# Ahead of each gather GpSimd waits for the memset two back instead of for the newest one

## What is computed

```python
sparse_embed = emb_tables[field_idx[None, :], x_sparse]          # 512 x 26 x 64
z = sparse_embed.reshape(B, N_FIELDS * K)
gram = jnp.einsum('bik,bjk->bij', sparse_embed, sparse_embed)
inner = gram[:, iu, ju]                                          # 325 pairs
dnn_in = jnp.concatenate([x_dense, z, inner], axis=-1)           # 512 x 2002
h = jax.nn.relu(dnn_in @ w1 + b1)
out = jax.nn.sigmoid(h @ w2 + b2)
```

## Time and profile before

| | us |
|---|---|
| median of 3 runs | 212.64 (212.23 to 212.67) |
| span of the profiled execution, first to last instruction | 209.4 |
| what lies around the span (median less span) | 3.2 |
| TensorE busy in the span | 200.7 |
| GpSimd busy in the span | 128.2 |
| time GpSimd's gathers sat idle behind the memset | 26.3 |

### The profile page before, as it was taken

How to read it: one execution, slowest core, us unless ns; L and a number is a source line. 1 busy time by engine, 2 the same in 40 slices (tenths; PEclk the granted TensorE clock), 3 DMA queues, 4 the chain that set the end, 5 groups by cost and what they waited for, 6 DMA issues and landing times.

```text
span 209.4 us, 3900 instructions
## 1 busy us (share of the span) xinstructions
PE 200.7 (96%) x1340; PEld 162.1 (77%) x1340; DVE 148.3 (71%) x346; ACT 129.7 (62%) x257; POOL 128.2 (61%) x210
## 2 busy tenths in 40 slices
PE   8999989699999999999999899999999999999993
PEld 8966867578777788876888688888888888788882
DVE  3666675498936779869668899574976897673473
ACT  2765464397937848977387736685999947542201
POOL 5887888888787887858878788878785000000000
PEclk9999999999999999999999999999999999999999
DMA  5388999977493831336786566978897178023100
GB/s 155 91 269 257 322 297 349 363 223 256 127 299 92 278 107 29 116 79 161 253 312 215 141 202 180 338 222 226 270 300 219 67 202 292 9 46 56 30 0 0
DMA packets 15388, 39.00 MB, mean 186 GB/s; under 512 B 3881, under 2 KB 5281, under 8 KB 15369
## 3 DMA queue, kind: packets, MB, share of 16 engines
q1 hardware_dynamic: 11688, 35.27, 52.0%
q0 software_dynamic: 3328, 3.41, 7.7%
q10 hardware_dynamic: 353, 0.08, 0.2%
HBM read 37.71 MB, written 0.69 MB: 183 GB/s over the span
## 4 chain that ended last, share of the span: by engine, by line
PE 65%; POOL 16%; DMA 6%; DVE 5%; issue 5%; ACT 2%; DVEq 0%; POOLq 0%; ACTq 0%
PE slot L1080 19%; PE slot L1083 18%; PE slot L1086 18%; POOL E L824 14%; DMA E<-emb,row_idx 5%; PE slot L1040 4%; PE slot L1070 2%; PE slot L1071 2%; PE slot L1072 2%; DVE G L978 2%; POOL pace L832 2%; DVE w_lo L930 1%; ACT w_hi L848 1%; DMA x_idx<-idx 1%; DVE slot L1004 1%
## 5 line engine op out<-in xcount | busy, mean ns | idle before, releaser
L824 POOL DMA_INDIRECT E<-emb,row_idx x104 | 110.5, 1063 | 31.7 <-POOL pace L832 26.3
L930 DVE TENSOR_TENSOR w_lo<-w_raw,w_hi 128x500 fp32r<-128x500 f32 (+6 forms) x128 | 80.2, 671 | 10.4 <-ACT w_hi L848 9.6
L848 ACT CAST w_hi<-w_raw 128x1000 fp32r<-128x1000 f32 (+6 forms) x64 | 65.5, 1029 | 27.3 <-DMA w_raw<-w 18.8
L1080 PE MATMUL slot<-w_hi,x_hi 128*128 128x500 f32 (+5 forms) x236 | 75.1, 399 | 3.6 <-ACT x_hi L874 2.6
L1083 PE MATMUL slot<-w_lo,x_hi 128*128 128x500 f32 (+5 forms) x236 | 72.8, 389 | 0.0
L1086 PE MATMUL slot<-w_hi,x_lo 128*128 128x500 f32 (+5 forms) x236 | 72.6, 389 | 0.0
L1080 PEld LDWEIGHTS slot<-w_hi,x_hi 128*128 128x128 f32 (+2 forms) x236 | 43.0, 189 | 15.9 <-ACT x_hi L874 6.1
L1086 PEld LDWEIGHTS slot<-w_hi,x_lo 128*128 128x128 f32 (+2 forms) x236 | 44.5, 189 | 9.2
L1083 PEld LDWEIGHTS slot<-w_lo,x_hi 128*128 128x128 f32 (+2 forms) x236 | 44.5, 189 | 9.2
L879 ACT COPY ET<-T 32x128 f32<-32x128 f32 (+4 forms) x89 | 32.5, 366 | 2.0
L947 DVE STREAM_TRANSPOSE T<-E 128x256 f32<-128x256 f32 x24 | 10.6, 443 | 21.1 <-DMA E<-emb,row_idx 21.0
(11 more groups left out here) (39 smaller groups left out, 80.4 us busy)
## 6 DMA issues: line engine op xcount, KB each, us to landing
w_raw<-w SPq DMA_DIRECT2D x32, 501.0 KB, 5.2
w_raw<-w SPq DMA_DIRECT2D x32, 500.0 KB, 4.6
E<-emb,row_idx POOLq DMA_INDIRECT x104, 4.0
w_all<-w SPq DMA_DIRECT2D x1, 1001.0 KB, 7.3
gram_dram<-G SPq DMA_DIRECT2D x8, 84.5 KB
x_in<-gram_dram SPq DMA_DIRECT2D x8, 42.0 KB
x_in<-G SPq DMA_DIRECT2D x4, 58.5 KB
x_in<-G SPq DMA_DIRECT2D x4, 19.5 KB
```

The lines of the kernel that those rows point to most:

```text
L824: nc.gpsimd.indirect_dma_start(out=E[:, k % ER, j, :], out_offset=None, in_=emb_rows, in_offset=bass.IndirectOffsetOnAxis(ap=row_idx[:, at ...
L848: nc.scalar.copy(w_parts(m)[0], w_source(m)).then_inc(w_hi_ready, 1)
L930: nc.vector.tensor_tensor(lo[:, cols], w_source(m)[:, cols], hi[:, cols].bitcast(F32), ALU.subtract)\
L1080: nc.tensor.matmul(acc[q], xh, hi[:, cols[q]], start=first, stop=False)
```

## The change

Three edits. The tile `pace` gets two halves, used in turn. The wait on `paced` moves from behind the memset to ahead of it, and asks for the memset before the last one; so between a memset and the gather behind it there is no wait. And the planner's assumed time from gather to gather goes from 1.50 to 1.40 us.

```diff
             for _ in range(GROUP_GATHERS[ARRIVALS[k][1]]):
-                pool_at += 1.25 if k < 2 else 1.50
+                pool_at += 1.25 if k < 2 else 1.40
                 g_issued.append(pool_at)
...
-        pace = sb("pace", [P, PACE], F32)
+        pace = sb("pace", [P, 2, PACE], F32)
...
                     if at > SOON:
-                        nc.gpsimd.memset(pace[:], 0.0).then_inc(paced, 1)
-                        pool.wait_ge(paced, at - SOON)
+                        if at > SOON + 2:
+                            pool.wait_ge(paced, at - SOON - 2)
+                        nc.gpsimd.memset(pace[:, at % 2], 0.0).then_inc(paced, 1)
```

## The result

The changed kernel takes 210.41 us (median of 18 runs) against 212.41 of the kernel before in the same comparison; the ratio is 0.9909, with a 95% interval of 0.9886 to 0.9933. So it is faster by about 1.9 us, where 2.7 were forecast. The profiled execution has a span of 207.4 us, before 209.4. The ratios leave out executions that are over 1.5% above the fastest of their kernel, here mostly ones whose mean TensorE clock is 0.982 to 0.992, so for a kernel that often loses clock the ratio looks better than its median.

What follows compares the result with a forecast made beforehand. TensorE, busy 200.7 of 209.4 us, was taken as the bound, idling for late gather arrivals up to k11. Gains 1.5 (k4, k5) + 1.5 (later boundaries) - 0.3 (piece 34) = 2.7 us: 212.64 to 209.9, range 208.7 to 212.9, chance 0.53.

Steps and rivals of the forecast that it cites:

- The interval: GpSimd's quiet gather-to-gather time: from 1.39 to 1.285 us, a gain of 0.10 a gather, bounds 1.25 and 1.42.
- interval stays: Rival at GpSimd: the memset's 0.17 replaces the wait's cost, interval within 0.02 of 1.39; 212.6 us, chance 0.13.
- interval grows: Rival at GpSimd: the gather's 0.30 starts at the memset's end, each interval 0.03 longer; 213.8 us, chance 0.11.
- all of 0.27 goes: Last rival, at GpSimd: gathers follow memsets at once, 1.12 us apart; 208.5 us, chance 0.05.
- What it brings at k4 and k5: TensorE's waits for gather arrivals k4 (0.8 lost) and k5 (2.1 lost): earlier gathers win 1.5 us by k5.
- the landing doesn't move: Rival: the DMA queue, not GpSimd, sets when k4 and k5 land; first 1.5 us lost, 211.4 us, chance 0.18.
- k9 and k11: TensorE's waits at arrivals k9 and k11, bound by gathers: losses of 0.3 and 0.25 us go.
- k6 and k10: x_hi casts for arrivals k6 and k10 move ahead of a weight cast: losses of 0.36 and 0.4 us go.
- k8: Arrival k8, three weight casts staying ahead: about 0.35 of 0.5 us stays, 0.15 goes.
- the boundaries: TensorE's idle time where arrivals k6, k8, k9, k10 and k11 begin: 1.5 us won in sum.
- The new lists: Reordered operations from the planner's 1.40: k6 0.36, k10 0.4 and k8 0.15 us go, against 0.3 lost at piece 34.
- The loss: Two copies into X24 ahead of weight pieces 32 to 34 delay piece 34's w_lo: 0.3 us, bounds 0 and 0.5.

Runs made afterwards that it cites:

- e3: The changed kernel with memsets only behind the first eight paced gathers; ratio to the kernel before 0.9886 (0.9833 to 0.9939), quiet interval 1.25 us.
- e1: The changed kernel with the planner's old 1.50, so the new wait and halved tile with the old lists; ratio to the kernel before 0.9906 (0.9867 to 0.9945).
- e2: The kernel before with only the planner's number set to 1.40, so new lists with the old wait; ratio 1.0229 (1.0183 to 1.0275), 4.9 us slower.
- second trace: The changed kernel run again, unedited, on one chip with three other kernels; 210.54 us, ratio to the kernel before 0.994 (0.9904 to 0.9976).
- e7: The changed kernel with x_hi of (3,6) ahead of weight cast hi 38 in ScalarE's list; ratio to the kernel before 0.9891 (0.9854 to 0.9928).
- e4: The changed kernel with the 1 MB load of w2_all issued behind load 20 instead of load 12; ratio to the kernel before 0.9962 (0.9925 to 0.9998).
- e6: The kernel before with the 1 MB load of w2_all moved behind load 29; ratio to the unedited kernel before 1.0131 (1.0093 to 1.0169).
- e10: The changed kernel with x_hi of (3,6) ahead of hi 38, hi 54 moved earlier, few memsets, w2_all in its old place; 208.25 us, ratio to before 0.9831.

## Why the prediction was right, and where its sizes were off

*The interval* came out at 1.28 against 1.285 taken; both bounds (1.25 and 1.42) are excluded for the kernel as it is, and e3 shows the 0.30 as a start of the gather's own. The rivals "interval stays", "interval grows" and "all of 0.27 goes" fall by this one number. By the Trainium skill, "GPSIMD Engine Reference", section Instruction dispatch, completion of a Pool instruction does not hold back the next one. The trace agrees so far: at 1.28, and not 1.42, the gather's start of 0.30 is not held back until the memset has ended. The 1.12 that the last rival made of this rule left that start out. The advice of "Perfetto Trace Analysis" in the Trainium skill, section GPSIMD Engine Instruction, to go by start-to-start spacing, held: the spacing gave 1.285, the lengths 1.12.

*What it brings at k4 and k5* is the term that was mis-sized: 1.5 forecast, 0.9 in the trace (k5 from 38.45 to 37.57). The cause is that I used the quiet gain of 0.10 for every interval. From the 5th to the 20th gather the mean is (30.57 - 8.92) / 15 = 1.44 against 1.505, a gain of 0.06, since gathers in the dense stretch are often longer, like the 1.47 at 24.26, and more of them were here (8 of 15 over 1 us, before 6); the 20th starts at 30.57 and not at 30.05. That is 0.98 earlier than before, and its landing takes 0.1 longer (6.06 against 5.96), which makes the 0.9. Up to the 44th the mean is (64.37 - 8.92) / 39 = 1.42, a gain of 0.08. Executions differ by nearly as much as the whole term: the 20th gather starts at 30.35 to 31.65 in the four traces with the old wait, at 29.88 to 30.71 in the six with the new wait and all memsets.

The rival "the landing doesn't move" was right for k4 alone: k4's gathers, though out 0.4 us sooner (25.73 against 25.12 + 1.03), landed a microsecond later. VectorE's turning of k4 after:

```profile
31.01 0.45 DVE L948 STREAM_TRANSPOSE T<-E 128x256 f32<-128x256 f32 x1 [2.88 <-DMA E<-emb,row_idx]
```

And before:

```profile
29.98 0.45 DVE L947 STREAM_TRANSPOSE T<-E 128x256 f32<-128x256 f32 x1 [1.09 <-DMA E<-emb,row_idx]
```

I had said k4's idle time goes; it was 0.5 to 1.8 us in two traces. It took nothing from the 0.9: k5 begins as soon as its own arrival lets it. VectorE's turning and ScalarE's cast of k5 in the changed kernel:

```profile
36.63 0.45 DVE L948 STREAM_TRANSPOSE T<-E 128x256 f32<-128x256 f32 x1 [1.32 <-DMA E<-emb,row_idx]
37.11 0.41 ACT L875 CAST x_hi<-T 128x256 fp32r<-128x256 f32 x1 [2.43 <-DVE T L948]
```

The steps follow 0.46 behind the cast's start (37.57 - 37.11), as before (38.45 - 37.99). So the reason held: an earlier last gather brings k5 forward. How far it does is, by the load's effect above, also a matter of what lies beside it in the queue.

*k9 and k11* went as written: x_hi no longer comes last there, and k11 starts 2.3 earlier (3.0 forecast, the missing 0.7 being k5's 0.6 and 0.1 of boundaries). *k6 and k10* closed too, and k8 kept a rest of 0.27 beyond the pipelined start, close to the 0.35 that I left. So in the trace the boundaries gave 1.4 of 1.5.

*The new lists* were credited with k6, k8 and k10, 0.9 us of that, less 0.3. The places are right: k6 and k10 keep their delay in e1 and lose it with the new lists. In the end time this is not to be seen: e1 with the old lists has the same ratio as the whole change, and the intervals leave about 1 us either way, more than the 0.6 that the forecast had for the lists. That what a list gains in one place it keeps to the end was only argued, and no run here shows it. e2 says how sharp such lists are: planned for 1.40 and fed at 1.50 they lose 4.9 us.

*The loss* at piece 34 was put at 0.3. TensorE's idle time near there grew from 0.68 to 1.07, to 1.25 in the second trace, and what it waited for was mainly not w_lo of piece 34 but the x_hi behind weight cast hi 38, as e7 showed. In e1, where the copies into X24 stand as before, it was 1.35, so they aren't needed for it. Size about right, place right within 3 us, cause wrong.

Sum: 0.9 + 1.4 - 0.4 = 1.9, which is the 1.9 measured. Of the gain of 2.3 at k11 TensorE's last step keeps about 1.9. That the terms of one trace meet the median so well is partly luck: in the second trace k5 is 1.7 earlier than in the trace of before and k11 2.5, but gram 5 waits 0.84 us, and the span is 1.4 shorter (208.0). What holds beyond one trace is the direction, the place up to k11, and that the wait alone gives about the whole.

## What to carry to other kernels

A wait taken off one queue is worth its price per round times the rounds up to where the bound engine needs the result, and the price has to be taken from the stretch in which these rounds run, not from a quiet one. Behind it the next limit is a shared one: before counting on an earlier issue, look how long the transfers take from issue to landing in that stretch, and what large load lies beside them. A list that was ordered for assumed times should be re-measured apart from the edit whose times it assumes: here it paid nothing that could be measured with it, and lost 2.3% without.

## What the runs showed of the hardware

A long idle time of TensorE was not only its own length. In e4, behind 2.07 us:

```profile
55.20 0.71 PE L1081 MATMUL slot<-w_hi,x_hi 128*128 128x500 f32 x2 [2.07 <-ACT x_hi L875]
```

Some 2 us later (length, busy and matmuls begun, granted clock, DMA share, GB/s):

```profile
57.20:57.70 0.50, 0.50 (x3) 0.50 0.76 140
```

The granted clock is 0.50 of full speed, the lower of its two levels, 1.2 GHz instead of 2.4, and the pairs start 0.83 us apart (56.67, 57.50) instead of 0.455. The 4.5 us behind that idle time in e4:

```profile
55.20:59.70 4.50, 4.50 (x14) 0.66 0.58 183
```

And the 4.5 us behind the 1.84 us at k4 in the changed kernel:

```profile
31.95:36.45 4.50, 4.50 (x20) 1.00 0.98 329
```

Six matmuls are missing in e4, some 1.4 us on top of the idle time. The same stood behind 2.49 us (e1), and 2.76 (e2 at k4, and e3 near 116 us). Behind idle times of 1.2 to 1.95 us, fourteen in these traces, the clock stayed full; it also did behind 2.35 us in e6 and behind 2.27 in e2's last group. So idle times of over 2 us lost it four times out of six here, and what decides between them is open. In e7 to e10, whose traces show no idle time over 1.9 us, none of 24 executions had a mean clock below 0.996; of the kernel before it was 5 of 23, 6 of 16 and 6 of 19 in the three comparisons.
